# Second attention's scores from two fp32r parts, two heads in one tile of rows, and one maximum for two heads

## The reference, cut to what matters

```
H = 32; KV = 8; D = 16; REP = 4                    # second attention, B = 2, S = 512
q = _rope((x @ wq + bq).reshape(B, S, H, D))
k = _rope((x @ wk + bk).reshape(B, S, KV, D))      # each used by 4 heads
v = (x @ wv + bv).reshape(B, S, KV, D)
scores = einsum('bqhd,bkhd->bhqk', q, k) / sqrt(D)
probs = softmax(scores)
out = einsum('bhqk,bkhd->bqhd', probs, v)
```

## Time and profile before

| | |
|---|---|
| Runs, median (lowest to highest), 3 | 1672.77 us (1672.37 to 1676.54) |
| The profiled execution | 1669.84 us |
| Its span, first to last instruction | 1667.9 us |
| Granted TensorE clock, mean | 0.881 |
| PE busy | 1309.1 us (78%) |
| DVE busy | 1128.4 us (68%) |
| ACT busy | 674.6 us (40%) |
| POOL busy | 784.7 us (47%) |
| Costliest group | L1085, 256 maxima, 166.8 us |

### The profile page before, as it was taken

The page is one execution under the profiler, slowest core; times in us unless marked ns, Lnnn a source line. Parts: engine busy times, 40 slices in busy tenths (PEclk is TensorE's granted clock), DMA queues, the critical chain, the costliest instruction groups (busy, mean ns, idle before and its releaser), DMA issues. The chain is left out here.

```text
span 1667.9 us, 19815 instructions
## 1 busy us (share of the span) xinstructions
PE 1309.1 (78%) x6320; PEld 896.2 (54%) x6320; DVE 1128.4 (68%) x2511; ACT 674.6 (40%) x1275; POOL 784.7 (47%) x721
## 2 busy tenths in 40 slices
PE   2768999999999999999999995675998579873000
PEld 0547767767767767777777674454222542223000
DVE  5644665556655666555566657795886859888998
ACT  0323433433334334334334331116476355774642
POOL 2237656765665757567566566561001600004244
PEclk8889999999999999999999998886799758995555
DMA  5211122122122121211221112300000000000001
GB/s 170 57 54 39 51 75 73 49 70 83 51 64 77 51 70 57 71 44 58 64 63 52 51 53 105 126 1 0 2 2 1 1 1 1 2 1 1 1 13 38
DMA packets 68215, 76.91 MB, mean 46 GB/s; under 512 B 5944, under 2 KB 40056, under 8 KB 68112
## 3 DMA queue, kind: packets, MB, share of 16 engines
q1 hardware_dynamic: 66240, 72.92, 14.3%
q10 hardware_dynamic: 1872, 2.72, 0.4%
HBM read 73.15 MB, written 2.28 MB: 45 GB/s over the span
## 5 line engine op out<-in xcount | busy, mean ns | idle before, releaser
L1085 DVE TENSOR_REDUCE nm<-bank 128x1 f32<-128x512 f32 x256 | 166.8, 677 | 17.1 <-PE bank L657 16.7
L1332 ACT ACTIVATE yTh<-yF 128x512 fp32r<-128x512 f32 x64 | 40.4, 632 | 330.6 <-DVE yF L940 330.6
L1520 POOL TENSOR_TENSOR sw<-sw,sinT 128x512 f32<-128x512 f32 x80 | 103.1, 1288 | 139.9 <-ACT sw L1283 139.9
L1532 POOL TENSOR_TENSOR dec<-gb,gcol 128x512 f32<-128x512 f32 x64 | 70.7, 1105 | 204.8 <-DVE Sd L906 190.7
L548 PE MATMUL bank<-st,qt 128*128 128x128 f32 x384 | 83.0, 301 | 61.6 <-DVE Sd L906 46.0
L878 DVE SCALAR_TENSOR_TENSOR gs<-tg,bank 128x512 f32<-128x512 f32 x64 | 44.0, 688 | 117.8 <-ACT tg L1290 117.8
L496 PE MATMUL bank<-hTh,wgh 128*128 128x512 f32 x256 | 121.3, 474 | 0.0
L657 PE MATMUL bank<-ksT,qsT 96*128 96x512 bf16 x256 | 112.5, 449 | 8.3 <-DVE nm L1085 3.1
L496 PE MATMUL bank<-hTh,wqh 128*128 128x512 f32 x256 | 107.1, 419 | 0.0
L576 PE MATMUL bank<-woh,yTh 128*128 128x512 f32 x256 | 104.4, 408 | 2.7 <-DVE yTl L943 2.7
L548 PEld LDWEIGHTS bank<-st,qt 128*128 128x128 f32 x384 | 66.7, 211 | 71.1 <-DVE Sd L906 50.1
(11 more groups left out here) (298 smaller groups left out, 3701.8 us busy)
## 6 DMA issues: line engine op xcount, KB each, us to landing
gb<-g_scr SPq DMA_DIRECT2D x64, 256.0 KB, 3.5
raw<-in_wmod SPq DMA_DIRECT2D x40, 256.0 KB, 2.7
raw<-in_wo SPq DMA_DIRECT2D x32, 256.0 KB, 2.8
raw<-in_wq SPq DMA_DIRECT2D x31, 256.0 KB, 2.7
raw<-in_wg SPq DMA_DIRECT2D x31, 256.0 KB, 2.7
mt<-mods_scr SPq DMA_DIRECT2D x20, 256.0 KB, 6.9
stg<-in_wmod SPq DMA_DIRECT2D x2, 1024.0 KB
xin<-in_x SPq DMA_DIRECT2D x8, 256.0 KB, 7.2
```

The costliest lines, as they stand in the source:

```text
L1085: ve.tensor_reduce(nm[:, i, h:h + 1], banks[bk][:, :], AX.X, ALU.max, negate=True).then_inc(*v_nm.up(b, h, i))
L1520: po.tensor_tensor(s_[:, :], s_[:, :], sinT[:, :], ALU.mult).then_inc(*g_rope.up("sin", kind, t, n))
L1532: po.tensor_tensor(dec[:, :, :], gb[s % 2][:, :, :], bc(gcol[:, t % 2, heads(t), n], 2, 128), ALU.subtract).then_inc(*g_dec.up("sub", s))
```

## The change

Q and K are cut into two fp32r parts (high and low), and three combinations (high.high, high.low, low.high) make 48 rows for a head; 16 more rows stand beside them, zeros for Q and ones for K. So a head has 64 rows, and heads p and 16 + p share one tile of 128 rows (`g` = 0, 1). A pair of heads is turned by one plain fp32 transpose, four to a bank. `parts3` is gone. The maxima are cut into two fp32r parts and go by two DMAs to rows 48, 49 and 112, 113. `pass_a` makes two matmuls, one in each half of the rows, to two neighbouring banks, and one `tensor_reduce` takes both maxima. The groups of four heads are now pairs 2qd, 2qd+1 of both halves (`qd`). Banks: 0 to 3 for two pairs of maxima; 4, 5, 6 in turn (`spin`) for scores before the exponential, turned maxima, turned outputs, `turn_l` and `logits`; 7 for P.V. The line has 64 steps and 3; `ahead` takes two ticks with each step instead of one, and 16 steps are taken before the first exponential. The diff, cut to its core:

```diff
-    banks = [ctx.enter_context(nc.psum_tensor(f"bank{i}", [128, 512], F32)) for i in range(8)]
+    pairs = [ctx.enter_context(nc.psum_tensor(f"banks{2 * i}{2 * i + 1}", [128, 1024], F32)) for i in range(4)]
+    banks = [pairs[i // 2][:, i % 2 * 512:i % 2 * 512 + 512] for i in range(8)]
...
+        def spin(self):
+            self.nspin += 1
+            return (4, 5, 6)[(self.nspin - 1) % 3]
+
...
         def turn_part(self, i, n):
-            pe, j, z_ = self.e, i % 4, i % 2
-            bk = (6, 7, 0, 1)[(5 * j + n) % 4]
-            pv_ = banks[bk][:, :].bitcast(BF16)
-            src, h0 = (qs[z_], 8 * n) if n < 4 else (ks[z_], 0)
-            pe.wait_ge(*a_part("q3", i))
-            pe.wait_ge(*a_part("k3", i))
+            pe, z_, bk = self.e, i % 2, turn_bank(i, n)
+            src = flat(qs[z_] if n < 4 else ks[z_])
+            if i < 2:
+                pe.wait_ge(*v_aw("ones"))
+            pe.wait_ge(*v_part("q", i))
+            pe.wait_ge(*v_part("k", i))
             pe.wait_ge(*self.drain[bk])
-            for h in range(8):
-                mm = pe.transpose(pv_[0:96, h * 128:(h + 1) * 128], src[:, h0 + h, :], identb[:, :])
+            for m in range(4):
+                q = 4 * n + m if n < 4 else m
+                mm = pe.transpose(banks[bk][:, m * 128:(m + 1) * 128], src[:, 128 * q:128 * q + 128].bitcast(F32), ident)
             mm.then_inc(*p_part.up(i, n))
             self.drain[bk] = a_pt(i, n) if n % 2 == 0 else v_pt(i, n)
 
-        def pass_a(self, b, h, i):
-            pe, bk = self.e, (0, 1, 7)[self.npa % 3]
+        def pass_a(self, b, p, i):
+            pe, z_ = self.e, self.npa % 2
             self.npa += 1
-            if h == 0 and i == 0:
+            if p == 0 and i == 0:
                 for n in (1, 3):
                     pe.wait_ge(*v_pt(4 * b + 3, n))
                 for n in (4, 0, 2):
                     pe.wait_ge(*a_pt(4 * b + 3, n))
-            pe.wait_ge(*self.drain[bk])
-            pe.matmul(banks[bk][:, :], qsT[0:96, h, i * 128:(i + 1) * 128], ksT[0:96, h // 4, :], start=True,
-                      stop=True).then_inc(*p_a.up(b, h, i))
-            self.drain[bk] = v_nm(b, h, i)
-
-        def max_part(self, b, grp, part):
-            if part < 5:
+            for g in range(2):
+                pe.wait_ge(*self.drain[2 * z_ + g])
+                mm = pe.matmul(banks[2 * z_ + g], qsT[64 * g:64 * g + 48, p, i * 128:(i + 1) * 128], ksT[64 * g:64 * g + 48, p // 4, :],
+                               start=True, stop=True)
+                self.drain[2 * z_ + g] = v_nm(b, p, i)
+            mm.then_inc(*p_a.up(b, p, i))
+
+        def max_part(self, b, qd, part, bk):
+            if part < 2:
                 return
             pe = self.e
-            pv_ = banks[2][:, :].bitcast(BF16)
-            pe.wait_ge(*v_mx(b, grp, 4))
-            pe.wait_ge(*self.drain[2])
+            pe.wait_ge(*v_mx(b, qd, 1))
+            pe.wait_ge(*self.drain[bk])
             for i in range(4):
-                mm = pe.transpose(pv_[0:12, i * 128:(i + 1) * 128], nmp[:, i, :, :].rearrange("p a h -> p (a h)"), identb[:, :])
-            mm.then_inc(*p_mx.up(b, grp))
-            self.drain[2] = a_mT(b, grp)
-
-        def scores_b(self, b, kv, kt, h):
-            pe, bk = self.e, (3, 4, 5)[self.npb % 3]
-            self.npb += 1
-            if kt == 0 and h == 0:
-                pe.wait_ge(*d_mr(b, kv))
+                mm = pe.transpose(banks[bk][0:8, i * 128:(i + 1) * 128], nmp[:, i, :, :, :].rearrange("p g a h -> p (g a h)").bitcast(F32), ident)
+            mm.then_inc(*p_mx.up(b, qd))
+            self.drain[bk] = a_mT(b, qd)
...
-            pe.matmul(banks[bk][:, :], ksT[0:99, kv, kt * 128:(kt + 1) * 128], qsT[0:99, 4 * kv + h, :], start=True,
-                      stop=True).then_inc(*p_b.up(b, kv, kt, h))
-            self.drain[bk] = a_exp(b, kv, kt, h)
-
-        def pv(self, b, kv, kt):
+            pe.matmul(banks[bk], ksT[64 * g:64 * g + 50, p // 4, kt * 128:(kt + 1) * 128], qsT[64 * g:64 * g + 50, p, :], start=True,
+                      stop=True).then_inc(*p_b.up(b, qd, kt, pr, g))
+            self.drain[bk] = a_exp(b, qd, kt, pr, g)
...
         def memsets(self):
             ve = self.e
             ve.wait_ge(*g_x("a", 7))
-            ve.memset(ksT[96:99, :, :], 1.0).then_inc(*v_aw.up("ones"))
+            ve.wait_ge(*p_ffn(7))
+            for z_ in range(2):
+                ve.memset(qs[z_][:, :, 48:64].bitcast(F32), 0.0)
+                v = ve.memset(ks[z_][:, :, 48:64].bitcast(F32), 1.0)
+            v.then_inc(*v_aw.up("ones"))
...
         def parts2(self, i):
             ve = self.e
             rq, rk, qv, kv = part_views(i)
-            ve.wait_ge(*a_part("q1", i))
-            ve.tensor_tensor(rq, rq, qv[:, :, 0, :], ALU.subtract).then_inc(*v_part.up("q1", i))
-            ve.wait_ge(*a_part("k1", i))
-            ve.tensor_tensor(rk, rk, kv[:, :, 0, :], ALU.subtract).then_inc(*v_part.up("k1", i))
-
-        def parts3(self, i):
-            ve = self.e
-            rq, rk, qv, kv = part_views(i)
-            ve.wait_ge(*a_part("q2", i))
-            ve.tensor_tensor(rq, rq, qv[:, :, 3, :], ALU.subtract).then_inc(*v_part.up("q2", i))
-            ve.wait_ge(*a_part("k2", i))
-            ve.tensor_tensor(rk, rk, kv[:, :, 1, :], ALU.subtract).then_inc(*v_part.up("k2", i))
+            ve.wait_ge(*a_part("q", i))
+            ve.tensor_tensor(qv[:, :, 2, :], rq, qv[:, :, 0, :].bitcast(F32), ALU.subtract).then_inc(*v_part.up("q", i))
+            ve.wait_ge(*a_part("k", i))
+            ve.tensor_tensor(kv[:, :, 1, :], rk, kv[:, :, 0, :].bitcast(F32), ALU.subtract).then_inc(*v_part.up("k", i))
+
...
-            ve.wait_ge(*p_a(b, h, i))
-            ve.tensor_reduce(nm[:, i, h:h + 1], banks[bk][:, :], AX.X, ALU.max, negate=True).then_inc(*v_nm.up(b, h, i))
-
-        def max_part(self, b, grp, part):
-            ve, v = self.e, nm[:, :, 4 * grp:4 * grp + 4]
+            ve.wait_ge(*p_a(b, p, i))
+            ve.tensor_reduce(nm[:, i, p:32:16], pairs[z_][:, :].rearrange("p (g t) -> p g t", g=2), AX.X, ALU.max,
+                             negate=True).then_inc(*v_nm.up(b, p, i))
...
+        def out2(self, b, qd, bk):
+            ve = self.e
+            tv = banks[bk].rearrange("p (i g q d) -> p i g q d", i=4, g=2, q=2)
+            ov = hh[b][:, :, :].rearrange("p i (g q d) -> p i g q d", g=2, q=16)
+            ve.wait_ge(*p_oT(b, qd))
+            ve.reciprocal(rd[:, :, :], banks[bk].rearrange("p (i u d) -> p i u d", i=4, u=4)[:, :, :, 16]).then_inc(*v_out.up("r", b, qd))
+            ve.wait_ge(*v_out("r", b, qd))
+            for g in range(2):
+                inc = v_out.up("o", b, qd) if g else v_out.up("o0", b, qd)
+                ve.tensor_tensor(ov[:, :, g, 2 * qd:2 * qd + 2, :], tv[:, :, g, :, 0:16], bc(rd[:, :, 2 * g:2 * g + 2], 3, 16), ALU.mult).then_inc(*inc)
...
-            ac.activation(qv[:, :, 0:3, :], bc(rq, 2, 3), ACTF.Copy).then_inc(*a_part.up("q1", i))
-            ac.activation(kv[:, :, 0:4:3, :], bc(rk, 2, 2), ACTF.Copy).then_inc(*a_part.up("k0", i))
-            ac.activation(kv[:, :, 5, :], rk, ACTF.Copy).then_inc(*a_part.up("k1", i))
-
-        def parts2(self, i):
-            ac = self.e
-            rq, rk, qv, kv = part_views(i)
-            ac.wait_ge(*v_part("q1", i))
-            ac.activation(qv[:, :, 3:5, :], bc(rq, 2, 2), ACTF.Copy).then_inc(*a_part.up("q2", i))
-            ac.wait_ge(*v_part("k1", i))
-            ac.activation(kv[:, :, 1:5:3, :], bc(rk, 2, 2), ACTF.Copy).then_inc(*a_part.up("k2", i))
-
-        def parts3(self, i):
-            ac = self.e
-            rq, rk, qv, kv = part_views(i)
-            ac.wait_ge(*v_part("q2", i))
-            ac.activation(qv[:, :, 5, :], rq, ACTF.Copy).then_inc(*a_part.up("q3", i))
-            ac.wait_ge(*v_part("k2", i))
-            ac.activation(kv[:, :, 2, :], rk, ACTF.Copy).then_inc(*a_part.up("k3", i))
+            ac.activation(qv[:, :, 0:2, :], bc(rq, 2, 2), ACTF.Copy).then_inc(*a_part.up("q", i))
+            ac.activation(kv[:, :, 0:3:2, :], bc(rk, 2, 2), ACTF.Copy).then_inc(*a_part.up("k", i))
...
-                inc = d_mr.up(b, grp) if p == 2 else d_mr.up(b, grp, p)
-                sp.dma_start(qsT[96 + p:97 + p, 4 * grp:4 * grp + 4, :], mT[4 * p:4 * p + 4, :]).then_inc(*inc)
+            sp.wait_ge(*a_mT(b, qd))
+            for g in range(2):
+                inc = d_mr.up(b, qd) if g else d_mr.up(b, qd, 0)
+                sp.dma_start(qsT[64 * g + 48:64 * g + 50, 2 * qd:2 * qd + 2, :].bitcast(F32), mT[4 * g:4 * g + 4, :].bitcast(F32)).then_inc(*inc)
...
-            for h in range(4 * grp, 4 * grp + 4):
+            for p in (2 * qd, 2 * qd + 1):
                 for i in range(4):
-                    E.pass_a(b, h, i)
-                    if grp and k < 6:
-                        E.max_part(b, grp - 1, k)
+                    E.pass_a(b, p, i)
+                    if qd and k < 3:
```

(73 more changed lines are left out.)

153 lines of the change are left out of this document (66 added, 87 removed).

## The result

Six runs of the changed kernel have a median of 1686.34 us (1681.39 to 1688.87), six of the kernel before 1673.58 (1669.97 to 1676.54): a ratio of 1.0075, 95% interval 1.0056 to 1.0094. It is slower by 0.75%, where 1645 was forecast. The profiled execution took 1688.87 us (span 1686.8), 46.5 more than the 1642.4 of the sum.

A forecast was written before the change was run, and what follows sets the result against it. Batch 0 was taken as bound by a loop of waits between PE's in-order queue and DVE, batch 1 by DVE. Stage terms summed to -27.4 us, 1642.4 for the profiled execution, so median 1645; range 1625 to 1661.

The forecast's parts named there:

- Slower: with less to stream, PE's clock falls: Rival for the groups of both passes: lower clock, a group some 4 us longer, all twelve give 1693; chance 0.05.
- The prediction's own signs of being wrong: Batch 0 groups of 10.6 or above 13.5 us, clock below 0.9, maxima above 1.3, or turning above 45.
- the wait for the second split: In a batch 0 group, PE waits 1.3 us for DVE's second split of the maxima, the next four scores queued behind.
- Group, batch 0, 12.9 us: Both passes, batch 0: a new group takes 12.9 us against 13.17; six groups make the stage 3.0 us shorter.
- the walk: One new batch 0 group followed step by step from its first pair at 0 to the next group at 12.9 us.
- Group, batch 1: Both passes, batch 1: a group takes 13.9 us with little idle on DVE; the stage gets 3.8 us shorter.
- Exponentials alone, batch 1, 25.3 us: Batch 1's last attention stage: 22.9 us scaled by 32/29 scores to 25.3, +2.4.
- the turning of batch 0: Turning Q and K of batch 0: smaller memsets, fewer copies and subtractions, -15 us, between 9 and 18.
- the wait for batch 1's rows: Exponentials alone, batch 0: 5.9 us of waits for batch 1's rows go, so the stage gets 3.4 us shorter.
- the double ticks: Maxima ahead, batch 1: 32 Sinkhorn steps in 16 places, each second one costing 0.24 us, and some waits: +5 us.
- Pairs one after the other: Rival: the two matmuls of a pair don't overlap and cost 0.44 us; batch 0 groups 13.4, 1649 us; chance 0.17.
- DVE is the bound: Rival for batch 0: the walked stalls overlap, so a group takes 10.6 us, giving 1631; chance 0.13.

The follow-up runs named there:

- e10: Changed kernel with all 64 rows of a head in both passes instead of 48 and 50, the added rows changing no product: 1660.17 us.
- e3: Changed kernel with the turned maxima sent to PE with the fifth pair of a group instead of the third (late turn): 1661.93 us.
- e14: Kernel before the change with both passes on rows 0 to 47 instead of 96 and 99: 1718.89 us.
- e11: e10 with the turned maxima sent with the fifth pair of a group instead of the third: 1645.65 us.
- e16: e15 with the pairs of maxima also issued twice in batch 1: 1638.51 us.
- e15: e11 with each score of the last two groups (qd 6 and 7) issued twice: 1638.36 us.
- e6: e3 with the pairs of maxima issued twice: 1650.23 us.
- e13: e11 with the pairs of maxima issued twice: 1648.57 us.

## Why the prediction was wrong

**The step that failed** is "Slower: with less to stream, PE's clock falls", set at 0.05 because the exponentials alone kept clock 1.00 in the kernel before. It was the right mechanism and the right price ("some 4 us" a group: it was 17.0 on the mean in batch 0 against 13.6 at full clock, 3.4). The prediction's own signs of being wrong, a clock below 0.9 and groups above 13.5 in batch 0, both came. I weighed it by time of streaming and by one stage, and missed the quantity that the change halves: each pass had 96 or 99 rows at work for 0.22 us a head, now 2 x 48 or 2 x 50 rows for 0.22 us a pair of heads. In batch 0 the rows were the larger part: 64 instead of 48 and 50 took 17.4 us off its two stages (e10), the late turn alone 6.5 (e3). In batch 1 64 rows alone took off 3.4 us, none of it in the stage with both passes, and the wait for the second split was the larger part: without it the two stages are 15.4 us shorter (e3). The row that I held against it, exponentials alone in batch 1, says nothing of the groups, and the same table has 0.89 for them in batch 0: in e14 the stage of batch 1 keeps 1.00 with 48 rows too (21.7 us), while the groups before it lose their clock.

**Group, batch 0, 12.9 us.** Mis-sized by itself: with the wait of PE it is 13.6 at full clock (e10), 0.4 longer than before and not 0.3 shorter. The stall was found (0.79 us of waiting where I had 1.3), but what follows it was walked too short. With the turned maxima at 3.1 as in the walk, e10's group from 1218.64 has P.V 0 at 5.3, P.V 1 at 8.1, P.V 2 at 11.6 and the next group at 13.6; the walk had 5.1, 7.8, 10.9 and 12.9. Which wait stretches each step is open. Without the wait for the second split the group is 12.87 (e11), DVE idle for 2.7 of it. Group, batch 1: 13.9 forecast, 14.25 at full clock.

**The two stages together** then account for the miss: (24.9 + 6.4) + (21.2 + 1.4) = 53.9 us above forecast. The start of the span adds 5.9, the turnings, the maxima ahead and the end give back 13.3: 46.5.

**Exponentials alone, batch 1, 25.3 us.** At clock 1.00 they take 29.4 us with each score issued twice (e16), and no run has them at 1.00 with single scores. In batch 0 the doubled stage takes 30.6 (e15) and the single one 28.0 (e6), so the forecast is too low by some 1.5 us (an estimate, 29.4 less those 2.6) to 4. I scaled by scores, 32 for 29; but now ten P.V lie behind the last pair, where there were eight. What this stage gains in length the one before loses: both together take 113.2 us in e15, where the forecast's 88.4 + 25.3 make 113.7.

**Right:** the turning of batch 0 (-16.8 for -15; the four memsets take 0.48 and 0.17 us twice), the maximum of 1024 columns,

```profile
L1094 DVE TENSOR_REDUCE nm<-banks 128x2 f32<-128x1024 f32 x128 | 153.4, 1216 | 45.7 <-PE banks L672 45.6
```

1.216 us for 1.21, the pairs at once, PE's wait for the second split, the wait for batch 1's rows, which is gone (28.0 us for the stage in e6, at clock 1.00, for 26.8). The turning of batch 1 gained 13.9 for 10, and the double ticks cost 0.1 where I had 5. "Pairs one after the other" was not the case, "DVE is the bound" not in batch 0 (DVE is busy 10.2 us of a group's 12.87 in e11).

**Still open:** why more rows alone brought back the clock of batch 0 and not that of batch 1 (e10), and what the clock wants in exponentials alone: with 48 rows in the kernel before (e14) it fell to 0.58 in batch 0 and stayed at 1.00 in batch 1, and in e13 it ended at 0.71 in batch 1 where e16, with its scores there twice, had 1.00. Why e10 spreads over 23 us I only suppose: from one run to the next the clock falls in more or fewer groups (its mean goes from 0.866 to 0.883 as the time falls from 1666.82 to 1643.62).

## What to carry to other kernels

Where a change makes matmuls fewer or narrower, ask before anything else whether PE's clock survives it, and price the groups at both levels; a stage that holds the clock today holds it with today's rows. If a tile has spare rows that are zero on one side, take them into the matmul: that was 26 us for no instruction, most of them in one batch only, so look at each stage for itself. And in an in-order queue put a transpose that needs another engine's last step behind the work that is already ready: 24 us for one step moved.
